# Three small moves in a four-layer kernel: a weight load two heads later, stores on another queue, one-hot matrices built in pairs

## The reference

```python
x = x + _L0_attn_ref(_layernorm(x), Wq, bq, Wk, bk, Wv, bv, Wo, bo)   # 16 heads of 32, causal, softmax
x = x + _L0_ffn_ref(_layernorm(x), gate_w, w_gate_proj, w_up_proj, w_down_proj)
x = x + _L1_attn_ref(_layernorm(x), w_in, w_param, w_out)             # a chunked state-space scan
x = x + _L1_ffn_ref(_layernorm(x), lut, gate_idx, up_idx, down_idx)   # weights looked up in a table of 16

# _L0_ffn_ref, the mixture of experts: 32 experts of width 192, 8 per token
sel_w, sel_e = jax.lax.top_k(router_logits, 8)
masked = zeros((T, 32)).at[rows, sel_e].set(softmax(sel_w))
h = silu(x @ gate.T) * (x @ up.T) * masked
out = sum over experts of h @ down.T
```

## Time and profile before

| what | us |
|---|---|
| median of 3 runs | 2504.35 |
| lowest and highest of the 3 | 2496.16, 2515.22 |
| the profiled execution's own time | 2502.53 |
| its span, first to last instruction | 2501.0 |
| TensorE busy (share of the span) | 2293.1 (92%) |
| VectorE, ScalarE, POOL busy | 1468.3, 983.4, 1083.8 |

### The profile page before, as it was taken

How to read it: one execution, slowest core, us unless ns; L and a number is a source line. 1 busy time by engine, 2 the same in 40 slices (tenths; PEclk the granted TensorE clock), 3 DMA queues, 4 the chain that set the end, 5 groups by cost and what they waited for, 6 DMA issues and landing times. The chain is left out here.

```text
span 2501.0 us, 45740 instructions
## 1 busy us (share of the span) xinstructions
PE 2293.1 (92%) x12487; PEld 1756.7 (70%) x12488; DVE 1468.3 (59%) x3444; ACT 983.4 (39%) x2232; POOL 1083.8 (43%) x976
## 2 busy tenths in 40 slices
PE   7987999978559999999999499999899998999998
PEld 5863555537349899899899378887766565788886
DVE  6444666645665555555555557998076665655554
ACT  3124666652444444444444332222265553312111
POOL 3118888877025666666667111111176662000000
PEclk9988999999659999999999799999999999999999
DMA  5468999987549999999998624456497841000001
GB/s 180 124 190 319 346 360 349 359 329 284 219 139 228 275 281 270 264 273 272 251 253 145 191 86 168 160 176 206 142 258 182 202 102 39 13 26 26 25 10 68
DMA packets 256541, 487.08 MB, mean 195 GB/s; under 512 B 32369, under 2 KB 149489, under 8 KB 246674
## 3 DMA queue, kind: packets, MB, share of 16 engines
q1 hardware_dynamic: 190418, 267.84, 35.0%
q0 software_dynamic: 62976, 212.42, 30.3%
q10 hardware_dynamic: 3024, 5.29, 0.6%
HBM read 588.77 MB, written 198.66 MB: 315 GB/s over the span
## 5 line engine op out<-in xcount | busy, mean ns | idle before, releaser
L1499 PE MATMUL m_ps_u<-m_ring,m_xT_hi 128*128 x1280 | 371.0, 351 | 0.2 <-DVE m_xT_lo L1611 0.2
L1467 POOL DMA_INDIRECT expert_sum<-x_res,token_of x160 | 257.7, 1611 | 184.0 <-DMA expert_sum<-x_res,token_of 75.5
L1499 PEld LDWEIGHTS m_ps_u<-m_ring,m_xT_hi 128*128 128x128 f32 x1280 | 237.2, 190 | 1.0 <-issue 0.6
L838 ACT ACTIVATE probs<-ps_c 128x512 f32<-128x512 f32 (+3 forms) x384 | 176.5, 491 | 151.5 <-PE ps_c L764 108.8
L1499 PE MATMUL m_ps_u<-m_ring,m_xT_lo 128*128 x640 | 217.4, 340 | 0.0
L1460 POOL DMA_INDIRECT m_xg<-x_rows,token_of x160 | 172.5, 1078 | 100.6 <-issue 92.6
L1946 PE MATMUL s_ps<-s_x_hi,s_w_hi 128*128 128x512 f32 x512 | 200.6, 392 | 3.2 <-POOL s_w_lo L1916 3.2
L1946 PE MATMUL s_ps<-s_x_lo,s_w_hi 128*128 128x512 f32 x512 | 200.0, 391 | 0.0
L1946 PE MATMUL s_ps<-s_x_hi,s_w_lo 128*128 128x512 f32 x512 | 199.8, 390 | 0.0
L1625 DVE SCALAR_TENSOR_TENSOR m_h<-m_silu,m_xg,m_ps_u 128x128 f32<-128x128 f32 x160 | 55.6, 348 | 236.5 <-ACT m_silu L1564 180.7
L2715 DVE TENSOR_TENSOR x_res<-f_ps_o,x_res 128x512 f32<-128x512 f32 x176 | 109.3, 683 | 143.7 <-PE f_ps_o L2608 143.7
(11 more groups left out here) (364 smaller groups left out, 5674.5 us busy)
## 6 DMA issues: line engine op xcount, KB each, us to landing
m_ring<-w_split SPq DMA_DIRECT2D x160, 1536.0 KB
m_ring<-w_split SPq DMA_DIRECT2D x160, 768.0 KB
w_split<-e_gu_parts POOLq DMA_DIRECT2D x32, 1536.0 KB, 7.7
proj<-s_out SPq DMA_DIRECT2D x32, 1024.0 KB, 4.0
e_raw_gu<-w_experts POOLq DMA_DIRECT2D x32, 768.0 KB
w_split<-e_dn_parts POOLq DMA_DIRECT2D x32, 768.0 KB, 7.3
e_raw_dn<-w_experts POOLq DMA_DIRECT2D x32, 512.0 KB
q_st<-q_parts SPq DMA_DIRECT2D x32, 256.0 KB, 7.1
```

The lines of the kernel that those rows point to most:

```text
L838: nc.scalar.activation(probs[a][j % RING][:, :width], ps_c[(j * BATCH + a) % BUFS][:, :width], ACT.Exp, scale=SCALE).then_inc(exp_done, 1)
L1467: pool.indirect_dma_start(acc[j % 2], rows_at(j), y[j % TURNS], None, bounds_check=PADDED - 1, oob_is_err=True, compute_op=ALU.add).then_i ...
L1499: last = nc.tensor.matmul(ps_u[b % 2][:, :W_UP], x[b % 2][:, k, :], ring[:, first + k * GU_ROW:][:, bass.ds(place, W_UP)], start=(n == 0), ...
```

## The change

Four edits:

1. The low parts of q and k are stored from ScalarE's queue (`store_lo`). The store of step n - 1 stands in ScalarE's list behind `high_qk(n)`, with a wait for the low part of step n - 1; the last one stands at the end. POOL makes the last four low parts of the weights without stores in between.
2. POOL waits at the start of `attend` until all low parts are made, because the masks that it writes next share memory with the projection's buffers.
3. SP loads the second half of `wo` at the fourth head (`u == 3`), no longer at the second.
4. In `dispatch` the 8 choices are laid out as 4 pairs, and the two of a pair lie next to each other in memory for each place or block. The numbers of the places are written out twice (`places` is 128 x 160 x 2, filled by ScalarE). VectorE makes a 0/1 matrix `marked` of 128 x 1024 for each tile with one comparison, and `in_block` with another; ScalarE multiplies `marked` by the token's number for all 16 tiles. TensorE reads every second element. The odd tiles' path with `Abs` and `Relu` is gone, and so are two small operations on VectorE and one conversion.

```diff
@@ -342,11 +342,8 @@
 
             for n in range(2 * KD):
                 split_w(n)
-            for n in range(len(STEPS)):
-                pool.wait_ge(lo_done, n + 1)
-                pool.dma_start(home(n, 1), lo[:, n % BUFS, :].bitcast(F32)).then_inc(lo_stored[n % BUFS], 16)
-                if n < KD:
-                    split_w(2 * KD + n)
+            for n in range(2 * KD, 3 * KD):
+                split_w(n)
 
         @block.tensor
         def _(pe):
@@ -402,6 +399,10 @@
                 act.wait_ge(var_done, p + 1)
                 nc.scalar.activation(std[:, pair(p)], var_eps[:, pair(p)], ACT.Sqrt).then_inc(std_done, 1)
 
+            def store_lo(n):
+                act.wait_ge(lo_done, n + 1)
+                act.dma_start(home(n, 1), lo[:, n % BUFS, :].bitcast(F32)).then_inc(lo_stored[n % BUFS], 16)
+
             def high_w(n):
                 act.wait_ge(w_loaded[n % STAGES], 16 * (n // STAGES + 1))
                 nc.scalar.copy(part_of(w_hi, n), stage[n % STAGES][:, :]).then_inc(w_hi_done, 1)
@@ -417,6 +418,8 @@
                     act.wait_ge(hi_stored[n % BUFS], n // BUFS * 16)
                     act.wait_ge(lo_done, n - BUFS + 1)
                 nc.scalar.activation(hi[:, n % BUFS, :], ps[n % PS][:, :], ACT.Identity, bias=bias[:, m:m + 1]).then_inc(hi_done, 1)
+                if n > 0:
+                    store_lo(n - 1)
 
             for p in range(2):
                 deviations(p)
@@ -438,6 +441,7 @@
                     high_w(2 * KD + u - 1)
             for n in range(MT, len(STEPS)):
                 high_qk(n)
+            store_lo(LAST)
 
         @block.vector
         def _(dve):
@@ -555,6 +559,7 @@
 
         @block.gpsimd
         def _(pool):
+            pool.wait_ge(projected.lo_done, projected.all_done)
             pool.memset(mask[:, :], 0.0).then_inc(masked, 1)
             pool.memset(mask_T[:, :], 0.0).then_inc(masked, 1)
             pool.memset(marks[:, :BATCH], 1.0).then_inc(masked, 1)
@@ -697,7 +702,7 @@
             sp.wait_ge(projected.v_added, TILES)
             load_wo(0)
             for u in range(HEADS):
-                if u == 1:
+                if u == 3:
                     sp.wait_ge(wo_split, 2)
                     load_wo(1)
                 if u + E < HEADS:
@@ -1214,18 +1219,20 @@
 def dispatch(nc, weight, chosen, x_rows, meta, block_meta, token_of, pads_ready, shared, ring, w_split, gu_loaded, dn_loaded):
 
     E, C, RT, B = EXPERTS, BLOCK_COLS, 8, 4
+    PAIR = 2
+    PAIRS = TOP_K // PAIR
     assert N_TOK <= 2048 and max(BLOCKS, SLOTS) <= 2048
     with ExitStack() as ctx:
         sb = lambda n, s, dt=F32: ctx.enter_context(nc.sbuf_tensor("d_" + n, s, dt))
         chosen_bf, before, ones = sb("chosen_bf", [P, TILES, E], BF16), sb("before", [P, P], BF16), sb("ones", [P, P], BF16)
         token_i, block_i, fill_i, turn_i = sb("token_i", [P, TILES], I32), sb("block_i", [P, C], I32), sb("fill_i", [P, PER_EXPERT], I32), sb("turn_i", [P, RT], I32)
         token, block_no, fill, turn_at, one = sb("token", [P, TILES]), sb("block_no", [P, C]), sb("fill", [P, PER_EXPERT]), sb("turn_at", [P, RT]), sb("one", [P, E])
-        places_i, places, pad_i, pad_row = sb("places_i", [P, BLOCKS], I32), sb("places", [P, BLOCKS], F16), sb("pad_i", [P, 1], I32), sb("pad_row", [P, 1])
+        places_i, places, pad_i, pad_row = sb("places_i", [P, BLOCKS], I32), sb("places", [P, BLOCKS, PAIR], F16), sb("pad_i", [P, 1], I32), sb("pad_row", [P, 1])
         slot, slot_taken, top, slot_i = shared.take([TILES, E]), shared.take([TILES, E]), sb("top", [P, TILES, TOP_K]), sb("slot_i", [P, TILES, TOP_K], I32)
         block_of_i, place_of_i = sb("block_of_i", [P, TILES, TOP_K], I32), sb("place_of_i", [P, TILES, TOP_K], I32)
-        block_of, place_of, token_neg = sb("block_of", [P, TILES, TOP_K], F16), sb("place_of", [P, TILES, TOP_K]), sb("token_neg", [P, TILES])
+        block_of, place_of = [sb(n, [P, TILES, TOP_K], F16) for n in ("block_of", "place_of")]
         in_block, at_place = [shared.take([TOP_K, BLOCKS], F16) for b in range(B)], [sb(f"at_place{b}", [P, TOP_K, SLOTS], F16) for b in range(B)]
-        apart, place_neg = [sb(f"apart{b}", [P, TOP_K, SLOTS], F16) for b in range(2)], sb("place_neg", [P, TILES, TOP_K])
+        marked = [sb(f"marked{b}", [P, TOP_K, SLOTS], F16) for b in range(2)]
...
-        NEAR_TILES = [i for i in range(TILES) if i % 2 == 0]
-        FAR_TILES = [i for i in range(TILES) if i % 2 == 1]
+        in_pairs = lambda t: t[:, :, :].rearrange("p (q two) w -> p q (two w)", two=PAIR).rearrange("p q (w two) -> p q w two", two=PAIR)
+        choice = lambda t, k: in_pairs(t)[:, k // PAIR, :, k % PAIR]
+        numbers = lambda w: places[:, :w, :].unsqueeze(1).to_broadcast([P, PAIRS, w, PAIR])
+        pairs_of = lambda t, i, w: t[:, i, :].rearrange("p (q two) -> p q two", two=PAIR).unsqueeze(2).to_broadcast([P, PAIRS, w, PAIR])
 
         @block.gpsimd
         def _(pool):
@@ -1263,15 +1272,14 @@
 
         @block.scalar
         def _(act):
-            act.wait_ge(places_ready, 2)
-            for n, i in enumerate(FAR_TILES):
-                for k in range(TOP_K):
-                    last = nc.scalar.activation(apart[n % 2][:, k, :], places[:, :SLOTS], ACT.Abs, bias=place_neg[:, i, k:k + 1])
-                last.then_inc(apart_done, 1)
-                act.wait_ge(apart_done, n + 1)
+            act.wait_ge(constants, 5)
+            nc.scalar.copy(places[:, :, :], places_i[:, :].unsqueeze(2).to_broadcast([P, BLOCKS, PAIR])).then_inc(places_spread, 1)
+            act.wait_ge(converted, 6)
+            for i in range(TILES):
+                act.wait_ge(mark_done, i + 1)
                 if i >= B:
                     act.wait_ge(tokens_summed, i - B + 1)
-                nc.scalar.activation(at_place[i % B][:, :, :], apart[n % 2][:, :, :], ACT.Relu, scale=token_neg[:, i:i + 1], bias=token[:, i:i + 1]).then_inc(far_place_done, 1)
+                nc.scalar.activation(at_place[i % B][:, :, :], marked[i % 2][:, :, :], ACT.Copy, scale=token[:, i:i + 1]).then_inc(at_place_done, 1)
 
         @block.sync
         def _(sp):
@@ -1301,13 +1309,10 @@
                 last = nc.tensor.matmul(ps_rank[:, i + 1:, :], ones[:, :], chosen_bf[:, i:i + 1, :].to_broadcast([P, after, E]), start=False, stop=(i == TILES - 2))
             last.then_inc(ranked, 1)
             for i in range(TILES):
-                if i in NEAR_TILES:
-                    pe.wait_ge(near_place_done, NEAR_TILES.index(i) + 1)
-                else:
-                    pe.wait_ge(far_place_done, FAR_TILES.index(i) + 1)
+                pe.wait_ge(at_place_done, i + 1)
                 pe.wait_ge(in_block_done, i + 1)
                 for k in range(TOP_K):
-                    last = nc.tensor.matmul(ps_token[:, :], at_place[i % B][:, k, :], in_block[i % B][:, k, :],
+                    last = nc.tensor.matmul(ps_token[:, :], choice(at_place[i % B], k), choice(in_block[i % B], k),
                                             start=(i == 0 and k == 0), stop=(i == TILES - 1 and k == TOP_K - 1))
                 last.then_inc(tokens_summed, 1)
 
@@ -1316,10 +1321,10 @@
             nc.vector.tensor_copy(chosen_bf[:, :, :], chosen[:, :, :]).then_inc(chosen_ready, 1)
             nc.vector.memset(one[:, :], 1.0).then_inc(converted, 1)
             dve.wait_ge(constants, CONSTANTS)
-            for dst, src in ((fill, fill_i), (places, places_i), (token, token_i), (block_no, block_i), (turn_at, turn_i), (pad_row, pad_i)):
+            for dst, src in ((fill, fill_i), (token, token_i), (block_no, block_i), (turn_at, turn_i), (pad_row, pad_i)):
                 nc.vector.tensor_copy(dst[:, :], src[:, :]).then_inc(converted, 1)
 
-            dve.wait_ge(converted, 7)
+            dve.wait_ge(converted, 6)
             dve.wait_ge(counted, 1)
             nc.vector.tensor_copy(count[:, :], ps_count[:, :]).then_inc(planned, 1)
             dve.wait_ge(planned, 1)
@@ -1349,8 +1354,6 @@
             nc.vector.tensor_single_scalar(place_of_i[:, :, :], slot_i[:, :, :], SLOTS - 1, ALU.bitwise_and).then_inc(placed, 1)
             nc.vector.tensor_single_scalar(block_of_i[:, :, :], slot_i[:, :, :], SLOTS.bit_length() - 1, ALU.logical_shift_right).then_inc(placed, 1)
             dve.wait_ge(placed, TILES + 5)
-            nc.vector.tensor_scalar_mul(token_neg[:, :], token[:, :], -1.0).then_inc(places_ready, 1)
-            nc.vector.tensor_scalar_mul(place_neg[:, :, :], place_of_i[:, :, :], -1.0).then_inc(places_ready, 1)
             nc.vector.tensor_copy(place_of[:, :, :], place_of_i[:, :, :]).then_inc(places_ready, 1)
             nc.vector.tensor_copy(block_of[:, :, :], block_of_i[:, :, :]).then_inc(places_ready, 1)
 
@@ -1384,17 +1387,15 @@
             dve.wait_ge(planned, 20)
             nc.vector.tensor_scalar_mul(meta_i[:, 1, :], meta_i[:, 1, :], float(SLOT)).then_inc(plan_ready, 1)
 
-            dve.wait_ge(places_ready, 4)
+            dve.wait_ge(places_ready, 2)
```

(12 more changed lines are left out.)

4 lines of the change are left out of this document (2 added, 2 removed).

## The result

| | us |
|---|---|
| before, median of 20 runs | 2505.53 (2496.16 to 2517.38) |
| changed, median of 20 runs | 2511.95 (2504.22 to 2520.82) |
| ratio, 95% interval | 1.0028 (1.0014 to 1.0041) |
| the changed kernel's profiled span | 2513.7 |

The forecast was 2489.7, range 2476 to 2502. The change makes the kernel about 7 us slower.

What follows compares the result with a forecast made beforehand. Attention was taken as bound by POOL's chain, dispatch by VectorE. Terms 0 - 0.7 - 14.9 + 1.0 = -14.6 from the profiled 2502.5 gave 2487.9; 1.8 for the median made 2489.7 us, range 2476 to 2502.

Steps and rivals of the forecast that it cites:

- The bound: Attention: POOL's 440.2 us chain of 32 experts and two wo splits stays and sets the block's end.
- edit 3 at 0 us: Attention: loading wo two heads later removes SP's 24.7 us wait but gains 0 us on the path, -3 to +1.
- The first rival: Attention gives its 25 us after all, POOL's chain shrinking too: up to 24.7 us less, 2465; chance 0.07.
- a tie: Attention's end: POOL's last stores land at about 620 us and VectorE's last additions end at 620.2, the same microsecond.
- The stores on ScalarE's queue: Projection: moving the low parts' stores off POOL shifts everything up to POOL's start by -0.7 us, range -1.6 to +1.5.
- The early part: Projection step 4: TensorE's 1.67 us wait for POOL's low part of the weights goes, up to -1.5 us.
- the step that sized the landing: Projection's end: step 28's store lands between 161.8 and 163.0, taking 10.5 us like high parts or 11.7 like POOL's.
- none delivered, the later landing: Projection's worst case: none of step 4's 1.5 us gain arrives and the last stores land later, +1.5 us.
- The one-hot matrices: Dispatch: VectorE at double rate takes 1.36 us per tile instead of 2.3, so the block ends 14.9 us earlier.
- the rival of a middle rate: Dispatch: a tile takes 2.1 us, by VectorE or TensorE's doubled products; block ends some 3 us earlier, 2500; chance 0.06.
- the single rate: Dispatch: VectorE at one element per cycle, 2.55 us per tile, 2507; chance 0.09 together with TensorE doubled.
- The gather beside SP's batch: After dispatch: POOL's first gather, issued amid SP's second batch of expert weights, costs +1 us, between 0 and 3.6.

Runs made afterwards that it cites:

- pool_stores: Changed kernel with low parts stored by POOL as before, later wo load and paired one-hot matrices kept: 2482.82 us, 0.993 of before.
- late_2: Repeat of high_by_head on another chip, second half of wo loaded at the fourth head: 2483.43 us, 0.9917 of before.
- early_2: late_2 with the second half of wo loaded at the second head, as before the change: 2478.07 us, 0.9905 of before.
- wo_early: Kernel before with only the paired one-hot matrices; POOL stores low parts, wo's second half loaded at the second head: 2487.0 us, 0.9952 of before.
- fill_8: pool_stores with eight useless VectorE comparisons added at the end of dispatch: one run, 2497.36 us, beside one of before at 2490.97.
- pool_2: Repeat of pool_stores on the chip of late_2: 2484.22 us, 0.9934 of before.
- high_by_head: Changed kernel with each high part stored in four DMAs of one head from SP's queue: 2477.25 us, 0.9927 of before.
- low_by_head: Changed kernel with each low part stored in four DMAs of one head from ScalarE's queue: 2490.75 us, 0.9955 of before.

## Why the prediction was wrong

*The bound, and edit 3 at 0 us: right as far as the runs can tell.* SP's wait is gone, TensorE's side runs ahead, and POOL's 440 us set the end. The first rival, attention giving its 25 us, fell. What the prediction called a tie had a small lead for POOL: where POOL is the last, the next block's first operation stands 7.0 us behind its last issue (642.67 to 649.64; 7.1 and 7.0 in `pool_stores` and `late_2`), where VectorE is, 1.3 behind its last addition (`early_2`, 624.97 to 626.24). Before, it stood at 623.46, 7.2 behind the one and 3.3 behind the other, so POOL led by 2 us. In `wo_early` TensorE's side was the last by some 10 us; the prediction held the tie for fixed.

*The stores on ScalarE's queue, -0.7 with +1.5 as the worst: wrong, by 26 us, and nearly the whole miss is here.* Measured at POOL's start +25.9. The early part was right in kind: TensorE's wait for the split is gone, and the fifth `qk_hi` starts at 44.16 in place of 47.10 (-2.9, foretold -1.5; 1.1 of it stood already at the first, 24.49 for 25.61). What failed is the step that sized the landing: the high parts, "stored from a hardware queue", took "10.5 us; POOL's took 11.7". It took the landing of one store on a queue that it had for itself, and gave the second stream on hardware the same, as if the capacity were the sixteen engines', of which a share of 0.49 was in use. The bound "+1.5 (none delivered, the later landing)" let the added stream cost nothing in every one of 32 steps. What a row could have told: 128 packets of the high parts in each step of 4.08 us, and in the DMA view of the kernel before, q1 with 21.0% of 16 engines for 1312 packets: the time of 3.4 engines. Whether those were four engines, nearly full, the pattern's outermost size of 4 said, in the order of instructions itself (`4x32x512`), with the section of the Trainium skill named above, which I did not weigh. With it a second stream of the same size doubles the load: 64 packets on each engine in a step, at the 102 ns of before 6.5 us, at the 82 ns measured since 5.2, against 4.08. In the trace the 18 steps from the fourteenth `qk_hi` to the last took 92.4 us (86.53 to 178.90) where they took 73.4, +18.9; the first thirteen had used up the early gain, +1.2; and from the last `qk_hi` to POOL's first load are 23.1 us for 17.3, +5.8, with POOL held by the landing of the last high part (idle 16.92). SP issues that part's store some 8 us behind the last `qk_hi`, after its first loads of q and k: at 167.26 before, at 186.99 now. From there to POOL's start were 8.8 us and are 15.0: 6.2 more, less 0.4 by which the issue stands closer to the last `qk_hi`. Together +25.9.

*The one-hot matrices, -14.9: right.* The durations 0.69 and 0.82 us were foretold to 0.01. From the attention block's end (VectorE's first operation of the next) to the first gather are 103.8 us before, 90.1 in the changed kernel and 88.4 in `pool_stores`: -13.7 and -15.4. TensorE's eight products of every second element took 0.75 at clock 1.00, and in `fill_8`, where the last eight ran at 0.51, 1.25: as long as the products of neighbours before at 0.50 (1.23 to 1.25), so reading with a step of two cost it nothing; the rival of a middle rate and the single rate both fell.

*The gather beside SP's batch, +1 (0 to 3.6): right in kind, too small.* 7.86 against 3.62, +4.2, above even the upper bound, and `fill_8` shows its cause.

*The sum.* +25.9 - 13.7 + 4.2 = +16.4 at the experts' first product (747.71 against 730.98 is +16.7; the rest is POOL's chain, 440.7 for 440.2); the medians are 6.4 apart. Behind that product the code is the same, but the stretch to the end took 1770.0 us in the one profile of before, 1766.0 in the changed kernel's and 1751 to 1767 in the others'. Two executions of one kernel already differ by 9 to 11 us there: 1754.6 and 1763.3 (`pool_stores` and `pool_2`), 1752.4 and 1763.1 (`high_by_head` and `late_2`). So a single profile is no measure for it, and where the 10 us between the trace's +16.7 and the medians' +6.4 went is not shown. The two halves by medians do add up: +25 (14 to 37) for the stores alone, -17 (11 to 24) for the rest, +7 together.

The chance of 2% for slower by over 1% named "a price that no row shows, such as a ScalarE that holds TensorE in every step". That mechanism did not occur: TensorE's own waits in the projection name VectorE (`qk_lo`, 6.8 us in all) and none names ScalarE. But another in the same place did, the landings; with the stores alone (1.0102) it would have come true. That the whole stayed within 1% is luck: the one-hot matrices' gain happened to cover a part of a loss that the prediction did not have.

## What to carry to other kernels

Before a stream is moved to another queue, read the shape of its DMA: if the outermost size is small, it runs from SP's and ScalarE's queues on as few engines, the same for both, and the mean share hides that these are full. Check the time per step as packets per engine times the time of one packet (82 to 102 ns for the 2 KB packets of one such store here), for all streams that fall on the same engines. Where two chains end a block in the same microsecond, shortening one gives nothing that runs can tell, though its trace looks 25 us better.

## What the runs showed of the hardware

- A 2 KB packet from SBUF to DRAM took 82 ns of its engine in the changed kernel, and on the mean of a queue's packets 102 in the kernel before and 128 for the stores by head of `low_by_head`; stores of 256 KB with outermost size 4, from SP's and ScalarE's queue together, were held to 102 GB/s, one step in 5.13 us.
- Comparisons of 16-bit numbers whose operands repeat in runs of two ran at (0.82 - 0.69) / 256 = 0.5 ns per element, half of the 1.04 of the earlier trace rows. The prediction asked whether the rule of the Trainium skill, "Vector Engine (DVE) Microarchitecture Reference", section 5.2, on hops of every element counts a repeated pair as such a hop, at 1.73 ns a pair: no such slower rate appeared.
- Four DMA issues in a row took ScalarE 2.0 us or 3.4 to 5.1 us in turn, not a steady 0.5 each (`low_by_head`).
- Products that read every second 16-bit element took as long as those of neighbours, 1.25 and 1.23 to 1.25 us for eight at clock 0.5.
- An indirect gather issued while 2.3 MB of other loads were under way reached TensorE 7.86 us after its issue, where it took 3.62 without them.
